# One PSUM bank freed for a tile that ScalarE and VectorE split: a feature-interaction tower on one Trainium2 core

## What is computed

```python
def _cin(x, weights, biases):
    B, F, D = x.shape
    hidden = x
    ...
    for i, (w, b) in enumerate(zip(weights, biases)):
        size = w.shape[0]
        z = jnp.einsum('bhd,bfd->bhfd', hidden, x).reshape(B, hidden.shape[1] * F, D)
        y = jnp.einsum('bcd,oc->bod', z, w) + b[None, :, None]
        y = jax.nn.relu(y)
        if i != n_layers - 1:
            hidden, direct = (y[:, :size // 2, :], y[:, size // 2:, :])
        else:
            direct = y
        finals.append(direct)
    return jnp.concatenate(finals, axis=1).sum(-1)
...
h = jnp.concatenate([z, dense_ctx], axis=1)
h = jnp.maximum(h @ W_top1 + b_top1, 0.0)
h = jnp.maximum(h @ W_top2 + b_top2, 0.0)
y = h @ W_top3
```

## Time and profile before

| | us |
|---|---|
| median of three runs | 1070.34 (1069.71 to 1072.66) |
| the profiled execution | 1070.25, of which span 1068.5 |
| TensorE matmul busy | 1023.0 (96%) |
| TensorE weight loads | 649.2 (61%) |
| VectorE | 931.2 (87%) |
| GpSimd | 921.0 (86%) |
| ScalarE | 724.6 (68%) |

### The profile page before, as it was taken

One profiled execution on the slowest core, in us unless ns is written; L12 is line 12 of the kernel. 1 busy time (PEld: TensorE's weight loads), 2 busy tenths in 40 slices (PEclk: granted clock), 3 DMA queues, 4 the chain that ended last, 5 costly groups with the idle time before them and its releaser, 6 DMA issues.

```text
span 1068.5 us, 10631 instructions
## 1 busy us (share of the span) xinstructions
PE 1023.0 (96%) x3447; PEld 649.2 (61%) x3447; DVE 931.2 (87%) x610; ACT 724.6 (68%) x794; POOL 921.0 (86%) x300
## 2 busy tenths in 40 slices
PE   2299999999999999999999999999999999999999
PEld 1146556566666666666666666666666666666663
DVE  3079999999998999999999999999989888988881
ACT  5056666677767767776777677677777777777762
POOL 6528777799999999999999999999988988898980
PEclk9999999999999999999999999999999999999999
DMA  6488788778778777887787778777776687677630
GB/s 171 91 208 191 179 196 188 174 189 187 188 179 190 185 176 182 189 194 175 187 191 175 173 189 192 177 191 182 186 167 167 165 190 165 165 170 182 165 73 0
DMA packets 140633, 183.87 MB, mean 172 GB/s; under 512 B 55633, under 2 KB 56273, under 8 KB 140450
## 3 DMA queue, kind: packets, MB, share of 16 engines
q1 hardware_dynamic: 135986, 178.93, 70.7%
q0 software_dynamic: 4096, 4.20, 2.2%
q10 hardware_dynamic: 496, 0.06, 0.0%
HBM read 174.66 MB, written 8.39 MB: 171 GB/s over the span
## 4 chain that ended last, share of the span: by engine, by line
PE 94%; POOL 2%; issue 1%; DVE 1%; ACTq 1%; DMA 1%; ACT 0%; DVEq 0%
PE py L641 43%; PE py L657 16%; PE py L647 16%; PE py L648 16%; POOL emb L341 2%; PE py L662 1%; DVE zf L552 1%; ACTq L449 1%; PE py L676 0%; PE py L713 0%; PE pzS L713 0%; ACTq L221 0%; PE py L683 0%; DMA emb<-in_tbl,idx 0%; DMA idx<-in_ids 0%
## 5 line engine op out<-in xcount | busy, mean ns | idle before, releaser
L351 POOL TENSOR_TENSOR zl<-zf,zh 128x2048 fp32r<-128x2048 f32 x168 | 771.8, 4607 | 87.4 <-ACT zh L413 85.3
L552 DVE TENSOR_TENSOR zf<-xs,hid 128x2048 f32<-128x2048 f32 x256 | 582.9, 2282 | 50.7 <-ACT hid L428 46.8
L641 PE MATMUL py<-zf,wf 128*128 128x512 f32 x1080 | 485.1, 592 | 1.2 <-DVE zf L552 1.2
L413 ACT ACTIVATE zh<-zf 128x2048 fp32r<-128x2048 f32 x185 | 353.5, 1911 | 99.3 <-DVE zf L552 96.0
L641 PEld LDWEIGHTS py<-zf,wf 128*128 128x128 f32 x1080 | 204.3, 189 | 208.5 <-issue 194.7
L647 PE MATMUL py<-zh,wh 128*128 128x512 f32 x740 | 290.0, 392 | 1.3 <-ACT zh L413 1.3
L648 PE MATMUL py<-zh,wl 128*128 128x512 f32 x740 | 289.7, 392 | 0.0
L657 PE MATMUL py<-zl,wh 128*128 128x512 f32 x740 | 228.0, 430 | 0.0
L657 PEld LDWEIGHTS py<-zl,wh 128*128 128x128 f32 x740 | 139.4, 188 | 69.3 <-issue 46.6
L341 POOL DMA_INDIRECT emb<-in_tbl,idx x128 | 149.0, 1164 | 30.3 <-issue 25.5
L647 PEld LDWEIGHTS py<-zh,wh 128*128 128x128 f32 x740 | 139.0, 188 | 34.6 <-ACT zh L413 2.6
(11 more groups left out here) (79 smaller groups left out, 336.1 us busy)
## 6 DMA issues: line engine op xcount, KB each, us to landing
xs<-x_dram SPq DMA_DIRECT2D x512, 256.0 KB, 5.3
xs<-x_dram SPq DMA_DIRECT2D x504, 64.0 KB, 2.1
x_dram<-emb SPq DMA_DIRECT2D x66, 64.0 KB, 5.5
x_dram<-emb SPq DMA_DIRECT2D x22, 96.0 KB, 5.5
emb<-in_tbl,idx POOLq DMA_INDIRECT x128, 4.5
x_dram<-emb SPq DMA_DIRECT2D x4, 384.0 KB
xs<-in_L_rec_w SPq DMA_DIRECT2D x2, 512.0 KB, 4.6
xs<-in_L_rec_w SPq DMA_DIRECT2D x1, 1024.0 KB, 7.5
```

The source lines that it names most:

```text
L351: pool.tensor_tensor(zl[:, q], zf[:, s], zh[:, q].bitcast(F32), ALU.subtract).then_inc(lo["P"], 1)
L413: act.activation(zh[:, q], zf[:, s], ACT.Copy).then_inc(hi, 1)
L552: dve.tensor_tensor(zf[:, slot(u)], left, right, ALU.mult).then_inc(mult, 1)
L641: mm = pe.matmul(y, wf[:, w, h], zf[:, s, h], start=first and h == 0, stop=ends and h == T - 1)
```

## The change

Layer 1 gets a single bank, `py1`. The freed bank, `pzB`, takes tile 0 of one unit at a time: of D in groups 11 to 62, of P from 44 on, of C from 11 to 42 (`through_bank`). VectorE writes that tile's products to `pzB` and the other three to `zf`; ScalarE rounds the tile out of the bank (`high_bank`) and VectorE subtracts there (`low_bank`). For P and D, TensorE then has three whole tiles and three fast matmuls for the fourth (`main_own`, `late_own`); for C the tile's low part moves from GpSimd to VectorE, and mode V ends for groups 11 to 42.

S, its high and low part and the direct sum of layer 1 are made for two groups in one instruction, 64 rows each; a group's tail is a matmul of 64 rows instead of 128. The second factor of S is loaded for two groups by SP into `x0_pair`; the first, `xt_pair`, is copied by ScalarE into `pzS`, where VectorE multiplies in place.

```diff
-    if name == "C" and g < 43:
-        return "V" if g % 3 == 0 else "P"
     return "P"
+def through_bank(unit):
+    name, g = unit
+    return name == "P" and g > 43 or name == "C" and 11 <= g < 43 or name == "D" and 11 <= g < LAST
...
+def pair_groups(q):
+    if q == 0:
+        return 0, 0
+    return 2 * q - 1, min(2 * q, LAST)
...
-        py1 = ps("py1", [P, 2, N])
+        py1 = ps("py1", [P, N])
+        pzB = ps("pzB", [P, N])
...
-            load_xt(1)
+            load_xt_pair(1)
+            load_x0_pair(1)
             load_xe(0)
             load_x0(2)
             for g in range(G):
                 if g + 2 < G:
-                    load_xt(g + 2)
+                    if g % 2:
+                        load_x0_pair(g // 2 + 2)
+                    else:
+                        load_xt_pair(g // 2 + 2)
...
-                pool.tensor_tensor(zl[:, q], zf[:, s], zh[:, q].bitcast(F32), ALU.subtract).then_inc(lo["P"], 1)
+                first = 1 if through_bank(u) else 0
+                pool.tensor_tensor(zl[:, q, first:T], zf[:, s, first:T], zh[:, q, first:T].bitcast(F32), ALU.subtract).then_inc(lo["P"], 1)
...
+            def high_bank(u):
+                if not through_bank(u):
+                    return
+                act.wait_ge(bank_mult, NTH_BANKED[u])
...
+                act.activation(bank_parts(u)[0], pzB[:], ACT.Copy).then_inc(bank_hi, 1)
+
+            def copy_xt(q):
+                act.wait_ge(xt_pair_in, 64 * q)
+                act.wait_ge(s_lo, q)
+                act.activation(pzS[:], xt_pair[:], ACT.Copy).then_inc(xt_copied, 1)
...
                 if g + 1 < G:
                     finish_straight(g + 1)
+                    high_bank(("D", g))
                     finish_dir1(g + 1)
                     finish_swapped(g + 1)
...
+                if first:
+                    if NTH_BANKED[u] > 1:
+                        dve.wait_ge(bank_lo, NTH_BANKED[u] - 1)
+                    dve.tensor_tensor(pzB[:], left[:, 0], view(right, at, [[1, N]]), ALU.mult).then_inc(bank_mult, 1)
+                dve.tensor_tensor(zf[:, slot(u), first:T], left[:, first:T], view(right, at, [[0, T - first], [1, N]]), ALU.mult).then_inc(mult, 1)
...
+                dve.scalar_tensor_tensor(zS[:], pzS[:], low_rows[:], zS_high[:].bitcast(F32), ALU.mult, ALU.subtract).then_inc(s_lo, 1)
+
+            def low_bank(u):
+                if not through_bank(u):
+                    return
+                dve.wait_ge(bank_hi, NTH_BANKED[u])
+                high_part, low_part = bank_parts(u)
+                dve.tensor_tensor(low_part, pzB[:], high_part.bitcast(F32), ALU.subtract).then_inc(bank_lo, 1)
...
-                if name == "P" and g >= 2:
-                    pe.wait_ge(swapped, 3 * (g - 1))
-                    pe.wait_ge(sum1_done, g - 1)
+                if name == "P" and g >= 1:
+                    pe.wait_ge(swapped, 3 * g)
+                    pe.wait_ge(dir1_ready, g)
...
+            def main_own(u):
+
+                if through_bank(u):
+                    i = OWN.index(u[0])
+                    pe.wait_ge(bank_hi, NTH_BANKED[u])
+                    pe.matmul(bank(u), whB[:, i], zhB[:, i], start=False, stop=False)
+                    pe.matmul(bank(u), wlB[:, i], zhB[:, i], start=False, stop=False)
...
             def tail(k):
-                pe.wait_ge(s_lo, k + 1)
-                pe.matmul(py1[:, k % 2], wS[:], zS[:], start=False, stop=True).then_inc(y1_ready, 1)
+                q, half = pair_of(k)
+                rows = slice(H * half, H * half + H)
+                pe.wait_ge(s_lo, q + 1)
+                pe.matmul(py1[:], wS[rows, :], zS[rows, :], start=False, stop=True).then_inc(y1_ready, 1)
```

More of the change, by code:

```diff
@@ L84 @@
 NTH_SPLIT = {u: i + 1 for i, u in enumerate(SPLIT)}
+BANKED = [u for u in UNITS if through_bank(u)]
+NTH_BANKED = {u: i + 1 for i, u in enumerate(BANKED)}
+OWN = "PD"
+NTH_OWN = {u: i + 1 for name in OWN for i, u in enumerate(v for v in BANKED if v[0] == name)}
 NTH_LOW = {u: i + 1 for m in "PV" for i, u in enumerate(LOW[m])}
@@ L412, in high, with high_s @@
                     act.wait_ge(used_split, i - ZS)
[L413 to L419, removed]
+                first = 1 if through_bank(u) else 0
+                act.activation(zh[:, q, first:T], zf[:, s, first:T], ACT.Copy).then_inc(hi, 1)
+            def high_bank(u):
+                if not through_bank(u):
+                    return
+                act.wait_ge(bank_mult, NTH_BANKED[u])
+                if u[0] not in OWN:
+                    act.wait_ge(used_split, NTH_SPLIT[u] - ZS)
+                elif NTH_OWN[u] > 1:
+                    act.wait_ge(used_own[u[0]], NTH_OWN[u] - 1)
+                act.activation(bank_parts(u)[0], pzB[:], ACT.Copy).then_inc(bank_hi, 1)
[3 more added lines that the diff above has]
+                act.activation(pzS[:], xt_pair[:], ACT.Copy).then_inc(xt_copied, 1)
+            def high_s(q):
+                act.wait_ge(s_mult, q + 1)
+                if q >= 1:
+                    act.wait_ge(s_lo, q)
+                act.activation(zS_high[:], pzS[:], ACT.Copy).then_inc(s_hi, 1)
             def finish_straight(k):
@@ L425, in finish_straight, with place_sums_1 @@
                 else:
[L426 to L428 removed]
+                    act.wait_ge(w_low, 5)
+                act.activation(hid[0:H, 0], py1[0:H], ACT.Relu, bias=bias0[0:H]).then_inc(straight, 1)
+                act.activation(hid[H:P, 0], py1[0:H], ACT.Relu, bias=bias0[0:H]).then_inc(straight, 1)
             def finish_dir1(k):
[L431 removed]
+                if k >= 2:
+                    act.wait_ge(sum1_done, k // 2)
+                half = slice(H * (k % 2), H * (k % 2) + H)
+                act.activation(dir1[half, :], py1[H:P], ACT.Relu, bias=bias0[H:P]).then_inc(dir1_ready, 1)
+            def place_sums_1(c):
+                act.wait_ge(sum1_done, GC // 2 * (c + 1))
+                for odd in range(2):
+                    act.activation(view(zd, H * zd[:].ap[0][0] + P * c + NS * odd, [[2 * NS, GC // 2], [1, NS]], H),
+                                   sums1[H * odd:H * odd + H, H * c:H * c + H].rearrange("p (j b) -> p j b", b=NS),
+                                   ACT.Copy).then_inc(sums1_placed, 1)
             def finish_swapped(k):
@@ L463, in _ @@
             for g in range(G):
+                if g == 0:
+                    copy_xt(1)
                 high(("A", g))
                 if g + 1 < G:
-                    high_s(g + 1)
+                    high_bank(("P", g + 1))
+                    if g % 2 == 0:
+                        high_s(g // 2 + 1)
                     if g + 2 < G:
                         copy_x0(g + 2)
+                if g % 2 and g + 2 < G:
+                    copy_xt(g // 2 + 2)
+                high_bank(("C", g))
                 high(("C", g))
+                if g % GC == GC - 1:
+                    place_sums_1(g // GC)
                 if g >= 1:
@@ L620, in bank @@
             def bank(u):
[L621 removed]
+                return py1[:] if u[0] == "P" else py2[:, u[1] % 2]
             def main(u):
@@ L635, in main @@
                         pe.wait_ge(mult, NTH[u])
-                    for h in range(T):
+                    first_tile = 1 if through_bank(u) else 0
+                    for h in range(first_tile, T):
                         if u == ("P", 0) and h < T - 1:
@@ L640, in main @@
                             pe.wait_ge(mult, 1)
-                        mm = pe.matmul(y, wf[:, w, h], zf[:, s, h], start=first and h == 0, stop=ends and h == T - 1)
+                        mm = pe.matmul(y, wf[:, w, h], zf[:, s, h], start=first and h == first_tile, stop=ends and h == T - 1)
                     mm.then_inc(used_whole, 1)
```

162 lines of the change are left out of this document (112 added, 50 removed).

## The result

The changed kernel takes **1090.42 us** (median of 6 runs, 1089.93 to 1092.59) against 1070.26 (6 runs, 1069.32 to 1072.66) for the kernel before on the same chip: ratio 1.0189, 95% interval 1.0176 to 1.0202. It is slower by 20 us, where 11 us less were forecast, and it lies above the range.

A forecast was written before the change was run, and what follows sets the result against it. TensorE was taken to bound the kernel (1023.0 of 1068.5 us). Sum: 1070.25 - 12.5 (split tiles) + 0 (tails' shape) + 1.2 (start) = 1059.0 us; range 1056.5 to 1077, held at about 0.8.

The forecast's parts named there:

- The tails' new shape: All 64 tails, 64 rows between 128-row matmuls: charged 0; bounds 0 and 0.18 a tail (11.5 us), beyond them full emptying.
- The rival: TensorE empties around each tail: 1070.5 at 0.09 a switch (chance 0.17), 1079.5 or more with emptying (chance 0.19).
- pairs above 31.42: Shape rival's sign below group 11: two-group steps longer than the 31.42 us of the kernel before.
- its two prices with emptying: Shape rival's cost over 64 tails: 0.32 each, 20.5 us, giving 1079.5; with both weight loads exposed, some 1104.
- L617 and L717: Earlier switches to 16 columns and to 1: the first lost nothing, the second 0.09; both judged equally far, 0 taken.
- 1070.25 - 12.5: Profiled time before, less 72 split tiles of D and P at 0.174 us each on TensorE.
- 15.19 and 15.01: Forecast TensorE steps in us per group: groups 11 to 42, and from 44, against 15.36 before.
- start charge: Kernel start: four x0-pair issues ahead of other loads on SP delay the first C; 1.2 us charged (0 to 1.7).
- VectorE's 14.9: VectorE's mean work per group in both late stages, in us; claimed to stay under TensorE's step.
- ScalarE's 12.2: ScalarE's busy time per group, in us, up from 11.2 through two added bank copies.
- GpSimd's 14.9: GpSimd's work per group in 11 to 42, under TensorE's step by 0.27; rival that it binds: 1087, chance 0.04.
- the ring: VectorE-ScalarE turn from group 44, 15.05 us, level with TensorE's step; rival that it binds at 15.2: 1063, chance 0.08.

The follow-up runs named there:

- e2_pad: Changed kernel with 128-row tails, using two weight copies with zeros in the other group's half; memory place unchanged: 1066.38 us.
- e9_tail96: Kernel before with each tail cut to 96 rows (part of S's low products left out): 1070.63 us, ratio 1.0002.
- e5_half_tail: Kernel before with each tail cut to 64 rows (lower half of S's products left out), memory untouched: 1095.70 us, ratio 1.0238.
- e3_both: Changed kernel with zero-filled 128-row tails and `low_rows` widened from 4 to 64 bytes: 1052.84 us, ratio to before 0.9834.
- e1_align: Changed kernel with `low_rows` widened from 4 to 64 bytes per partition, tails still 64 rows: 1078.35 us, ratio to before 1.0075.
- e11_both64: e3_both with its streamed operands moved by 64 bytes, to the distance from the weights of the kernel before: 1057.54 us, ratio 0.9881.
- e17_shift128: Kernel before with 128 unused bytes between weights and streamed operands: 1077.68 us, ratio 1.0068.
- e4_shift32: Kernel before with 32 unused bytes ahead of its inputs, behind the weights: 1078.87 us, ratio 1.0077.
- e14_weights64: Kernel before with weights moved by 64 bytes and everything from the first inputs on by 2048: 1067.30 us, ratio 0.9973.
- e16_all32: Kernel before with weights and streamed operands both moved by the same 32 bytes: 1071.36 us, ratio 1.0005.
- e8_shift64: Kernel before with 64 unused bytes ahead of its inputs: 1076.65 us, ratio 1.0062.
- e18_shift224: Kernel before with 224 unused bytes between weights and streamed operands: 1079.21 us, ratio 1.0074.
- e13_shift192: Kernel before with 192 unused bytes ahead of its inputs: 1065.96 us, ratio 0.9963.

## Why the prediction was wrong

**The step that failed** is "The tails' new shape": between bounds of 0 and more I took 0. It costs 0.39 to 0.40 a tail: 24.0 us from e2_pad to after, 25.1 from e9_tail96 to e5_half_tail, and 25.5 from e3_both to e1_align, where the slower first passes behind each tail are counted too. The rival was named, with its signs (gaps around L813, equal in all stages, pairs above 31.42); the cost lies between its two prices with emptying, 20.5 and some 45. Two rows were weighed as equally far, L617 and L717. L717 was the nearer: the same 0.76 ahead of a late weight load stands at the tails. I read there only the 0.09 by which the start was late, and no matmul of the old shape follows in that row, so the way back could not be seen. The rule of the Trainium skill (TensorEngine Tiling (Array Packing), Key Properties), that changing the tiling mode drains TensorE, agrees with the runs, if 64 rows are such a mode and 96 are not: 64 rows cost 0.40, while 96 rows cost nothing. The Trainium skill's TensorE: Matmul & The Clock Gate (Why this matters for your kernels) says of a single matmul of 32 rows that it takes the time of one of 128. That can't be carried over to a tail of 64 rows between matmuls of 128: it costs 0.40 more.

**A term that the sum lacked** is the place in memory. The sum took the pace of the earlier trace rows over unchanged; but it belongs to a distance of 64, and the change makes it 224. Worth: e2_pad against e11_both64, which has the distance of before, 1066.38 - 1057.54 = 8.8 us. Nothing in the diff says so but the declarations of two small tensors behind the weights, `pair16` of 128 bytes and `low_rows` of 32: 64 + 128 + 32 = 224, and every other size that the change adds or takes away there is a multiple of 256. Either alone would have led to a slow place: 64 + 128 = 192 is that of e17_shift128, 64 + 32 = 96 that of e4_shift32. By the Trainium skill (TensorE: Matmul & The Clock Gate, Step-by-step: what each phase is for) loads of the next weights take no read bandwidth from the running matmul, having a port of their own. Read strictly, that leaves the weights' place no part in the pace; in e14_weights64 and e16_all32 it has one, and the measurement decides.

**What held.** With both taken out, e11_both64 runs at 1057.54; 1070.25 - 12.5 is 1057.75. Its steps are 15.20 and 15.04 (forecast 15.19 and 15.01). The forecast without its start charge was thus right to 0.2 us, which is closer than its terms, and in part luck: the 52 steps of e11_both64 (tails at 228.12 and 1015.29) save 798.72 - 787.17 = 11.6 us, and the rest of its gain lies at the start and the end. That 1057.5 + 8.8 + 24.0 gives 1090.3 proves nothing, since these are the differences on the way from e11_both64 to after. But the prices found on the kernel before give it as well: 1057.5 + 25.1 for the tail + 6.4 to 8.7 for a slow place (e8_shift64, e18_shift224) is 1089.0 to 1091.3. By steps: 15.19 + 0.39 + some 40 fast passes x 0.0043 = 15.75, measured 15.73. The 1.2 us at the start can be neither seen nor excluded. VectorE's 14.9 a group was 14.0, ScalarE's 12.2 was 12.0, GpSimd's 14.9 was 14.6; the ring from group 44 does not bind at 14.97, so it takes less than the 15.05 worked out.

## What to carry to other kernels

Where a kernel is bound by TensorE, keep all matmuls of a stream in one shape: a half-height matmul between full ones cost 0.40 us more here than the full pass of 0.23 that it replaced, and filling the missing rows with zeros gave that back. When a change adds or resizes any tensor, compare the pace of the unchanged matmuls before and after; here, weights and streamed operands at the same place modulo 256 bytes gave the best pace, and 192 unused bytes alone made the kernel before 3.8 us faster (e13_shift192 against 1069.77, the kernel before in the same series of runs). A row that shows a new shape only once, with nothing of the old behind it, bounds one switch, not two.

## What the runs showed of the hardware that was not expected

- The pace of fast 512-column matmuls depends on the distance between weights and streamed operand: 0.2267 us at 0 modulo 256 bytes, 0.2289 at 64, 0.2331 to 0.2335 at 32, 96, 128, 192 and 224. Whole f32 passes do not show it: (922.20 - 920.49) / 4 = 0.428 at the slow place against 0.430 in the earlier trace rows. That the load of the next weights and the stream disturb each other is the obvious reading, but it was only argued: no run here changed the one's timing without the other's.
- Behind fast passes the weight load of a 128-row tail begins one pass ahead of its matmul (917.86 and 918.09 in e2_pad), that of a 64-row tail together with it (both 923.41 after). The idle time of the loads before it is 0.36 behind fast passes and 0.76 behind whole ones; the cost came out alike, 0.39 and 0.40.
- A tail of 96 rows costs what one of 128 does (six passes of 1.79 around it in both), one of 64 costs 0.40 more.
